# Spreading a small projection over the blocks of a Mamba front phase, with wider GpSimd instructions and ScalarE copies

## The reference, cut to what matters

```python
def _mamba_layer(x, ...):                        # x: group-normed
    xn = (xf - mu) * rsqrt(var + EPS) * ln_w + ln_b
    x_in, z = split(xn @ in_proj_w.T)            # 512 -> 2 x 1024
    u = silu(causal_conv4(x_in) + conv_b)
    dt, B, C = split(u @ x_proj_w.T)             # 1024 -> 32, 16, 16
    delta = softplus(dt @ dt_proj_w.T + dt_proj_b)
    y = selective_scan(u, delta, -exp(A_log), B, C) + u * D_skip
    return (y * silu(z)) @ out_proj_w.T
# x = x + mamba(gn(x));  x = x + memory_layer(gn(x))
```

## Time and profile before

| | us |
|---|---|
| median of 3 runs | 4900.57 (4899.47 to 4906.98) |
| the profiled execution, its time | 4903.02 |
| its span, first to last instruction | 4901.3 |
| first phase in it | 49.6 to 1144.8 |
| PE busy, all phases | 4639.4 (95%) |
| DVE, POOL, ACT busy | 4118.8, 3376.0, 2973.6 |

### The profile page before, as it was taken

How to read it: one execution, slowest core, us unless ns; L and a number is a source line. 1 busy time by engine, 2 the same in 40 slices (tenths; PEclk the granted TensorE clock), 3 DMA queues, 4 the chain that set the end, 5 groups by cost and what they waited for, 6 DMA issues and landing times. The chain is left out here.

```text
span 4901.3 us, 120019 instructions
## 1 busy us (share of the span) xinstructions
PE 4639.4 (95%) x47164; PEld 2944.2 (60%) x47164; DVE 4118.8 (84%) x4354; ACT 2973.6 (61%) x6011; POOL 3376.0 (69%) x1680
## 2 busy tenths in 40 slices
PE   6999899995899999999999999999998899999999
PEld 5666666663455555555555555555554688887787
DVE  7888888877999999999999999999997667676332
ACT  2666666665777777767777777777764445453111
POOL 0667677775999999999999999999997222222000
PEclk9999999997999999999999999999999999999999
DMA  4444443334323332333233323332332111111453
GB/s 167 146 152 159 164 151 135 140 143 153 94 77 97 97 97 79 96 97 97 79 97 97 98 80 97 96 98 80 98 96 79 50 67 78 78 77 80 187 204 137
DMA packets 195578, 538.37 MB, mean 110 GB/s; under 512 B 15904, under 2 KB 15920, under 8 KB 186016
## 3 DMA queue, kind: packets, MB, share of 16 engines
q1 hardware_dynamic: 190000, 480.31, 29.7%
q0 software_dynamic: 5104, 51.35, 2.6%
HBM read 329.22 MB, written 202.38 MB: 108 GB/s over the span
## 5 line engine op out<-in xcount | busy, mean ns | idle before, releaser
L1047 POOL TENSOR_TENSOR sc_hc<-sc_hc,sc_c_rep 128x1024 f32<-128x1024 f32 x1024 | 2396.6, 2367 | 184.3 <-ACT sc_state L1060 182.0
L1248 DVE TENSOR_TENSOR_SCAN sc_hc<-l_m,sc_state,sc_ring 128x512 f32<-128x512 f32 x2048 | 2429.8, 1257 | 25.4 <-PE sc_ring L1171 17.6
L1092 ACT ACTIVATE l_m<-l1s_v,l_neg_a 128x512 f32<-128x512 f32 x2048 | 1351.9, 707 | 1.0 <-DMA l1s_v<-spill 1.0
L1171 PEld LDWEIGHTS sc_ring<-sc_diag,l1s_iota 64*64 64x64 f32 x32768 | 889.0, 133 | 699.5 <-issue 699.3
L1171 PE MATMUL sc_ring<-sc_diag,l1s_iota 64*64 64x128 f32 x32768 | 1102.3, 275 | 8.1 <-DVE sc_hc L1248 5.8
L1181 PE MATMUL sc_y_ps<-sc_hc,sc_fold 128*64 128x512 f32 x4096 | 997.4, 608 | 29.3 <-POOL sc_hc L1047 24.8
L1060 ACT ACTIVATE sc_state<-sc_hc 128x2 f32<-128x2 f32 x1024 | 206.0, 201 | 639.6 <-DVE sc_hc L1248 639.6
L923 PE MATMUL sc_o_ps<-l1s_et,l_sums 128*128 128x512 f32 x1024 | 557.5, 631 | 11.8 <-ACT l_count L913 11.8
L1503 POOL TENSOR_TENSOR l_count<-l_count,as_oh 128x1024 f32<-128x1024 f32 x64 | 182.4, 2850 | 507.0 <-DVE as_oh L1686 507.0
L1181 PEld LDWEIGHTS sc_y_ps<-sc_hc,sc_fold 128*64 128x64 f32 x4096 | 249.9, 136 | 414.6 <-issue 378.4
L71 PE MATMUL fr_mm<-fr_xn_hi,l0f_w_in_hi 128*128 128x512 f32 x1024 | 436.9, 427 | 27.0 <-DVE fr_delta L708 11.8
(11 more groups left out here) (186 smaller groups left out, 6539.4 us busy)
## 6 DMA issues: line engine op xcount, KB each, us to landing
sc_duz<-spill SPq DMA_DIRECT2D x128, 768.0 KB, 5.9
l1s_v<-spill SPq DMA_DIRECT2D x256, 256.0 KB, 4.0
spill<-fr_z SPq DMA_DIRECT2D x64, 512.0 KB, 2.8
spill<-fr_u SPq DMA_DIRECT2D x32, 1024.0 KB, 9.9
spill<-fr_du SPq DMA_DIRECT2D x32, 1024.0 KB, 4.3
spill<-fr_delta SPq DMA_DIRECT2D x32, 1024.0 KB, 6.4
sc_c_rep<-bc SPq DMA_DIRECT2D x128, 256.0 KB, 4.3
soft<-l1s_et SPq DMA_DIRECT2D x16, 2048.0 KB, 6.2
```

The costliest lines, as they stand in the source:

```text
L1047: nc.gpsimd.tensor_tensor(hc[:, p], hc[:, p], c_rep[:, 2 * q:2 * q + 2, :], ALU.mult).then_inc(s_hp, 1)
L1092: nc.scalar.activation(da[:, p % 4, r, :], delta[:, i % 2, p % 2, :], ACT.Exp, scale=keep.neg_a[:, c:c + 1]).then_inc(s_da, 1)
L1171: done = nc.tensor.matmul(to[:, :, k::4], dut[rows, i % 2, k, HALF * h:HALF * h + HALF], diag[rows, u, 4 * q + c:4 * q + 4:2, k, :], start ...
L1248: nc.vector.tensor_tensor_scan(hc[:, p, r, :], da[:, p % 4, r, :], ring[:, SLOT[at], r::2], state[:, i, 2 * p + r:2 * p + r + 1], ALU.mult ...
```

## The change

1. PE: z0 is projected directly after x0, ahead of dt 0 to 3 (the list `ORDER` follows). `project_x` is cut up: blocks 0 and 1 of u behind z5, 2 and 3 behind z6, 4, 5 and 6 behind z7, and block 7 behind x0 of the next chunk. z7's matmuls count up a new semaphore `s_read`, group by group.
2. ACT writes the high parts (`high`) behind keep_x of block 7, each when z7 has read its group; silu of u6 comes behind them and ahead of silu of z7. In a new chunk keep_x of block 0 and silu of z0 come first.
3. DVE's `split` writes the low parts only; convolution 0 comes ahead of the four max(dt, 0).
4. POOL handles two blocks with one instruction of 128x1024.

```diff
-    ORDER = [("x", 0)] + [("d", m) for m in range(4)] + [("z", 0), ("x", 1), ("z", 1), ("x", 2), ("z", 2)]
+    ORDER = [("x", 0), ("z", 0)] + [("d", m) for m in range(4)] + [("x", 1), ("z", 1), ("x", 2), ("z", 2)]
...
-                for m in range(KD):
-                    n = KD * g + m
+                for m in range(0, KD, 2):
+                    n = KD * g + m + 2
+                    two = slice(m, m + 2)
                     pool.wait_ge(s_r, 2 * g + m // 4 + 1)
                     pool.wait_ge(s_ln, 2 * g + m // 4 + 1)
-                    nc.gpsimd.tensor_tensor(du[:, m, :], du[:, m, :], r[:, m % 4, :], ALU.subtract).then_inc(s_c1, 1)
...
+                    nc.gpsimd.tensor_tensor(du[:, two, :], du[:, two, :], r[:, m % 4:m % 4 + 2, :], ALU.subtract).then_inc(s_c1, 2)
...
-                    nc.gpsimd.tensor_tensor(du[:, m, :], u[:, m, :], delta[:, m, :], ALU.mult).then_inc(s_du, 1)
+                    pool.wait_ge(s_dl, n)
+                    nc.gpsimd.tensor_tensor(du[:, two, :], u[:, two, :], delta[:, two, :], ALU.mult).then_inc(s_du, 2)
...
+            def high(g, before=None):
+                act.wait_ge(s_xn, g + 1)
+                for k in range(KC):
+                    if before is not None and k < KC - 1:
+                        act.wait_ge(s_read, (KC - 1) * before + k + 1)
+                    elif before is not None:
+                        act.wait_ge(s_mm, count(before, "z", KD - 1))
+                    nc.scalar.activation(xn[0][:, k, :], v[:, k, :], ACT.Copy).then_inc(s_xh, 1)
...
+                keep_x(g, 0, ends)
                 if not first:
                     copy_dt(g - 1)
-                keep_x(g, 0, ends)
+                silu_z(g, 0)
...
-                silu_z(g, 0)
                 keep_x(g, 1, ends)
...
+                keep_x(g, KD - 1, ends)
+                if after(1):
+                    high(g + 1, g)
+                silu_u(g, KD - 2)
+                silu_z(g, KD - 1)
                 silu_u(g, KD - 1)
...
+                project(g, "x", 0, first)
                 if not first:
-                    project_x(g - 1)
-                project(g, "x", 0, first)
+                    project_x(g - 1, KD - 1, KD)
+                project(g, "z", 0, first)
                 if not first:
                     pe.wait_ge(s_dt, g + 1)
                     project_dt(g - 1, 0, 4)
-                project(g, "z", 0, first)
...
+                    if m > 4:
+                        project_x(g, 2 * m - 10, 2 * m - 8)
+                project_x(g, KD - 2, KD - 1)
...
-                for k in range(KC):
-                    nc.vector.tensor_copy(xn[0][:, k, :], v[:, k, :]).then_inc(s_xh, 1)
...
+                conv(g, 0)
                 if not first:
                     for m in range(4):
                         positive(g - 1, m)
-                conv(g, 0)
```

More of the change, by code:

```diff
@@ L272, in front @@
         s_xn = w.sem("xn_done")
+        s_read = w.sem("xn_read")
         s_xh = w.sem("xn_hi_done")
@@ L283, in front @@
         s_xd = w.sem("xdbl_done")
-        s_one = w.sem("ones_set")
         s_dt = w.sem("dt_copied")
@@ L504, in main @@
                 silu_u(g, 1)
-                for m in range(3, KD):
+                for m in range(3, KD - 1):
                     keep_x(g, m, ends)
@@ L521, in _ @@
             root(0)
+            high(0)
             chunks(act, main)
@@ L575, in project @@
                                         [part[:, k, :] for part in xn], k == 0, k == KC - 1)
+                    if (kind, m) == ("z", KD - 1) and k < KC - 1:
+                        last.then_inc(s_read, 1)
                 last.then_inc(s_mm, 5 if first and (kind, m) in (("z", 0), ("z", 2)) else 1)
@@ L583, in project_dt, with project_x @@
                                      dt[row:row + RANK + 1, :], start=True,
[L584 to L588, removed]
+                                     stop=True).then_inc(s_mm, {0: 3, 4: 5}.get(m, 1) if ends else 1)
+            def project_x(g, first, last):
+                if first == 0:
+                    pe.wait_ge(s_dt, g + 1)
+                for m in range(first, last):
                     pe.wait_ge(s_u, KD * g + m + 1 + 2)
-                    last = nc.tensor.matmul(xd_ps[:], keep.w_xp[:, m, :], u[:, m, :], start=(m == 0), stop=(m == KD - 1))
-                last.then_inc(s_xd, 1)
+                    done = nc.tensor.matmul(xd_ps[:], keep.w_xp[:, m, :], u[:, m, :], start=(m == 0), stop=(m == KD - 1))
+                if last == KD:
+                    done.then_inc(s_xd, 1)
             def main(b, j, after, first):
                 g = b * NJ + j
+                project(g, "x", 0, first)
                 if not first:
-                    project_x(g - 1)
-                project(g, "x", 0, first)
+                    project_x(g - 1, KD - 1, KD)
+                project(g, "z", 0, first)
                 if not first:
@@ L623, in _ @@
             chunks(pe, main)
-            project_x(NG - 1)
+            project_x(NG - 1, KD - 1, KD)
             pe.wait_ge(s_dt, NG + 1)
@@ L635, in _ @@
             for row in (RANK, 64 + RANK):
-                nc.vector.memset(ones[row:row + 1, :], 1.0).then_inc(s_one, 1)
+                nc.vector.memset(ones[row:row + 1, :], 1.0).then_inc(s_zero, 1)
             dve.sem_inc(s_rs, 1)
@@ L676, in normalise, with split @@
                 nc.vector.tensor_tensor(v[:], v[:], over_blocks(rs), ALU.mult).then_inc(s_xn, 1)
[L678 to L681, removed]
-                for k in range(KC):
-                    nc.vector.tensor_copy(xn[0][:, k, :], v[:, k, :]).then_inc(s_xh, 1)
+            def split(g):
                 for k in range(KC):
@@ L772, in main @@
                         positive(g - 1, m)
-                conv(g, 0)
-                if not first:
                     rounded(g - 1, 0)
@@ L806, in main @@
                 if after(1):
-                    split(g + 1, g)
+                    split(g + 1)
             norm_v(0, 0)
```

14 lines of the change are left out of this document (6 added, 8 removed).

## The result

| | before | after |
|---|---|---|
| median, us | 4901.42 (4899.47 to 4906.98, 4 runs) | 4950.38 (4945.5 to 4956.19, 4 runs) |
| the profiled execution | 4903.02 | 4946.38 |
| first phase ends at | 1144.8 | 1187.6 |
| everything behind it | 3756.5 | 3757.1 |

The ratio is 1.0098, with a 95% interval from 1.0083 to 1.0112: slower by 49 us, where 17 were forecast. In the two profiled executions, 43.4 us apart, practically the whole difference lies in the first phase, which ends 42.8 us later.

A forecast was written before the change was run, and what follows sets the result against it. The prediction took a loop of waits through GpSimd, ACT and PE to bound the first phase. First half +8.1, second half +1.6, step between +5, ends +2.5: together +17 on 4903.0, which is 2.4 over the median: 4918 us, range 4882 to 4942.

The forecast's parts named there:

- abs 4: ACT's abs of dt block 4, behind silu of u0: forecast at t = 12.6 us after GpSimd's first instruction, before 9.66.
- x3: PE's block x3, which needs dt 4's bank read: forecast to begin at t = 13.95 us, before 11.1.
- the low parts free of GpSimd: DVE's low parts at the chunk's end: first ends at t = 49.6 us, after GpSimd ends at 45.
- the wait for u7 gone: Sign: PE's wait on ACT for u7 disappears; in the first half about 1 us waiting for low parts replaces it.
- The clock: PE at 1.2 GHz on x3 after short waits: costs 0 to 1.6 us a chunk, 0.7 taken, making PE's path 66.2.
- the prediction's path for PE: PE's chain through one chunk, from x3 at 13.95 to GpSimd's next start: 65.5 us before the clock term.
- the signs of being wrong: Wrong if abs 4 starts before t = 10.5, x_dbl still waits over 2 us, or low parts take over 3 us.
- 66.2 us by DVE's path: First half: convolution 7 ends at 48.9, first low part 49.6, x0 follows to 52.5; chunk 66.2 us.
- The step between the halves and the ends: Between halves, DVE's normalising instructions each wait longer for GpSimd, plus one add: +5 us; first and last chunks: +2.5.
- 2.8 us of PE time are lost there in each chunk: At x3: wide GpSimd instructions release u0 late, delaying silu u0, abs 4 and x3; 2.8 us a chunk.
- The loop as intended: Rival: GpSimd's loop alone sets the chunk, 63.1 us; 27 us faster, 4874; needs abs 4 by t = 9.7; chance 0.06.
- Low parts hit: Rival: DVE's low parts wait behind wide GpSimd instructions and hold x0; two hit, +3.6 a chunk, 4965 us; chance 0.09.

The follow-up runs named there:

- run 8: Run 4 plus 12 matmuls that nobody reads, placed in PE's wait ahead of dt's block 6; 4934.6 us, ratio 1.0065.
- run 4: Changed kernel with SP's stores of delta and delta*u blocks 4 to 7 moved ahead of the store of z6 and z7; 4948.6 us, ratio 1.0087.
- run 5: Changed kernel with the old turn on PE, ACT, DVE: x_dbl's eighth matmul ahead of x0, dt 0 to 3 ahead of z0; 5019.9 us, ratio 1.0239.
- run 9: Run 5 with SP's load of v ahead of B and C stores, and delta's second store ahead of z's last; 4894.9 us, ratio 0.9985.
- run 2: Kernel before the change with only the two-block (wide) GpSimd instructions added; 4902.5 us, ratio 0.9994.
- run 1: Changed kernel with GpSimd back at one block per instruction (narrow); 4920.6 us, ratio 1.0030.
- run 3: Changed kernel with silu of u0 moved behind the absolute values of dt 4 to 7 on ACT; 4922.8 us, ratio 1.0041.
- run 6: Kernel before the change with only the high parts of the next input moved to ACT; 4907.5 us, ratio 1.0015.

## Why the prediction was wrong

**Right.** The direction. GpSimd's price per instruction (2.40 for 2.37), its 45 us (46.06), silu of u0 at 11.4, abs 4 at 12.45, x3 at 13.8 to 14.7 for 13.95 (where the mean was not late), the low parts free of GpSimd (2.49 us for four), the wait for u7 gone. The first chunk took 66.8 us against a forecast of 66.3.

**The step that failed, "The clock": +0.7 us, mis-sized.** The prediction saw two short waits (3.3 and 0.8 us) and priced them by the one wait of the earlier trace rows, as half of 3.1 us at most. They came as 2.7 us for the mean and 2.7 ahead of the last dt block, and the low clock behind the second lasts 6.8 us in the four chunks that take 68.3. Filling that wait gave 17 us of the first phase (run 8 against run 4), on average 2.0 us a chunk in the second half and 2.8 between chunks with all of it and none. With it filled, the second half's chunk is 65.5 us: the prediction's path for PE without its clock term. So for the second half the path was right and the term for the clock was about three times too small. Against the forecast the second half came out 13.5 us too long (those four chunks 2.1 each, the one behind the step 5.2), the first 7.6, the step 1.6 and the ends 2.9. With this wait filled and the load of v moved (run 8) the first phase ends at 1168.1, where the forecast stood for 1162. None of the signs of being wrong that the prediction named occurred, and none of them looked at the clock.

**The first half: 66.2 us by DVE's path, also too low.** With the load on time and at most 3.4 us of low clock (run 8), its chunks still take 66.8 to 67.2 us. Where the 0.6 to 1.0 us come from stays open.

**A step that was missing: the load of v.** The prediction did not speak of SP's queue at all. It took the mean matmul to be as early as before in all chunks; it came at 3.9 in the first chunk, at 6.3 to 8.9 in the other five of the first half, and for the chunk behind the step at 11.3 (71.4 us, 5.2 over the forecast). Run 4 put it back to 3.9 by moving one pair of stores. That alone did not buy time, since PE then met the wait for silu of z2 and the low clock, so the load explains where PE waited rather than a separate sum. With the old turn the same lateness was worth 125 us (runs 5 and 9).

**The step between the halves and the ends.** +6.6 for +5, and +5.4 for +2.5; the first by the mechanism that was given (run 2, which has only the wide GpSimd, shows +7.0 for the step). Run 1, with narrow instructions, took 74.2 us there, two thirds of the way back.

**"2.8 us of PE time are lost there in each chunk".** As a reading of the width it was too simple. Run 2 loses the same 3 us at x3 and still has the shorter chunk, because PE had 4.0 us of slack ahead of u7. Nor is it x_dbl on PE's path that makes the loss count: run 9 has x3 at 14.0 to 14.8 and x_dbl spread, and takes 63.3. What makes it count is the new turn, and by its size z0 (2.8 us) ahead of dt. The prediction's own sum agrees: 65.5 less z0 is 62.7, the length of run 9's chunks at full clock. The prediction had all these in its sum, but did not ask what each part would do alone. The answer: width -3 us, inside the interval, high parts +5.6, spread +3.7, each alone; and the new turn +46 to +55, on top of the three and with the load out of the way. Without the width the three other parts cost 0.30% (run 1).

**The rivals.** None is what happened. "The loop as intended", 4874, needed abs 4 by t = 9.7. Run 3 makes that so in 4 of 13 chunks, at 9.0 or 9.1, and they take 63.6 to 63.9 us, near the 63.1 of that rival; in the other nine it comes later, and the whole takes 4922.8. So its condition was sound, and the changed kernel does not meet it. "Low parts hit" was wrong for the changed kernel but is what runs 1 and 6 show with narrow instructions (up to 6.0 us for four).

What stays open: run 3 is 17 us slower than the kernel before, and I did not separate how much of that is z0 ahead of dt and how much the load. The new turn was never put alone into the kernel before, and its orders on PE, ACT and DVE were never separated; that z0 on PE is what costs is read from traces and fits in size, but is not tested by itself. No run has the old turn, an early load and a step that does not throw the next chunk over the cliff.

## What to carry to other kernels

Before you move work off a wait, ask what that work was hiding: z0's block filled 2.7 us in which PE otherwise waited for silu of z2, and ahead of dt it was on the path twice, as its own 2.8 us and as an idle PE with a slow clock. Where DVE shares SBUF with long GpSimd instructions, what counts is which side of GpSimd's start a DVE group falls on; draw the distance of each such group to that start, and follow it back to the DMA that feeds it, as closely as the long path. Test the parts of a bundled change one by one, and in pairs: here three of the four were within 0.15% alone, and with the fourth they cost 1%, but only 0.3% when the width was taken out again.

## What was not expected of the hardware

- Twelve useless matmuls a chunk made the first phase 17.4 us shorter (1185.5 to 1168.1).
- Four tensor_scalar instructions on 128x512 with a single SBUF input took 1.91 us ahead of GpSimd's start and 9.45 us behind it, with GpSimd's instructions at 2.4 us; four subtractions of 128x512 took 2.49 us alone and 6.01 with narrow GpSimd instructions beside them.
- The phases that no edit touches took from 3755.6 to 3771.5 us in the 14 traces, a spread of 16 us that says nothing of the edits, so the end of the first phase is the closer look at them: run 2 was 8.3 us shorter there, and its median was the same as before. How far that end scatters between executions of one kernel was not measured.
